# Group 1 of a graph attention layer by seven products instead of whole ones, with the sums of M on VectorE

## The reference

```python
h = jnp.maximum(_layernorm(x, axis=-1), 0.0)
output = jnp.einsum('bni,io->bno', h, weight)
q = jnp.einsum('bni,io->bno', h, wq)
k = jnp.einsum('bni,io->bno', h, wk)
alpha = jnp.einsum('bno,bmo->bnm', q, k)
alpha = jnp.maximum(alpha, 0.0) * (adj != 0)
alpha = jax.nn.softmax(alpha, axis=1)
x = x + jnp.einsum('bnm,bmo->bno', alpha, output)
```

## Time and profile before

| | |
|---|---|
| median of 3 runs | 415.41 us (415.18 to 416.22) |
| the profiled execution | 415.38 us, its span 413.5 us |
| granted TensorE clock, mean | 0.999 |
| busy: PE, DVE, ACT, POOL | 405.9, 297.0, 277.7, 264.7 us |
| start of scores(0), the first after group 0's products | 44.67 us |
| start of group 2's first product | 73.81 us |
| start of group 3's first product | 99.16 us |
| a later period | 23.6 us |

### The profile page before, as it was taken

One profiled execution on the slowest core, in us unless ns is written; L12 is line 12 of the kernel. 1 busy time (PEld: TensorE's weight loads), 2 busy tenths in 40 slices (PEclk: granted clock), 3 DMA queues, 4 the chain that ended last, 5 costly groups with the idle time before them and its releaser, 6 DMA issues.

```text
span 413.5 us, 9484 instructions
## 1 busy us (share of the span) xinstructions
PE 405.9 (98%) x3581; PEld 322.1 (78%) x3581; DVE 297.0 (72%) x569; ACT 277.7 (67%) x590; POOL 264.7 (64%) x284
## 2 busy tenths in 40 slices
PE   8999999999999999999999999999999999999995
PEld 5444545879798897979798797979889797979883
DVE  5799789596767777676767777676777667656465
ACT  4749877576767677776776776776867777643534
POOL 0749896969395875849486775939577584910003
PEclk9999999999999999999999999999999999999999
DMA  8973868978969797896979598796988699393022
GB/s 290 370 102 72 208 112 222 251 169 198 196 195 195 226 151 211 201 217 171 180 237 180 134 235 210 195 208 179 187 248 162 159 213 236 41 186 103 2 103 101
DMA packets 161641, 75.03 MB, mean 181 GB/s; under 512 B 135360, under 2 KB 143808, under 8 KB 161600
## 3 DMA queue, kind: packets, MB, share of 16 engines
q1 hardware_dynamic: 161312, 73.94, 77.9%
q10 hardware_dynamic: 288, 0.52, 0.3%
HBM read 24.12 MB, written 16.78 MB: 99 GB/s over the span
## 4 chain that ended last, share of the span: by engine, by line
PE 78%; DVE 7%; POOL 6%; ACT 6%; issue 2%; DVEq 0%; ACTq 0%
PE bank L1136 10%; PE bank L1139 10%; PE bank L1138 10%; PE bank L1153 9%; PE bank L1154 9%; PE bank L1151 9%; PE s_bank L1167 3%; PE s_bank L1166 3%; PE s_bank L1165 3%; PE bank L1172 2%; PE bank L1174 2%; PE bank L1173 2%; POOL hn_lo L423 2%; ACT h L543 2%; DVE raw_stats L828 1%
## 5 line engine op out<-in xcount | busy, mean ns | idle before, releaser
L423 POOL TENSOR_TENSOR hn_lo<-h,hn_hi 128x512 f16<-128x512 f32 x64 | 74.6, 1177 | 51.3 <-ACT hn_hi L553 51.2
L543 ACT ACTIVATE h<-x_sb,shift,rstd 128x512 f32<-128x512 f32 x64 | 49.9, 803 | 21.8 <-POOL shift L418 21.8
L449 POOL TENSOR_TENSOR hn_lo<-s,hn_hi 128x512 f16<-128x512 f32 x56 | 63.1, 1160 | 0.3 <-ACT hn_hi L558 0.3
L1138 PE MATMUL bank<-hT_lo,mt_hi 128*128 128x256 f16 x224 | 61.1, 273 | 0.0
L1136 PE MATMUL bank<-hT_hi,mt_hi 128*128 128x256 f16 x224 | 61.1, 273 | 0.0
L1139 PE MATMUL bank<-hT_hi,mt_lo 128*128 128x256 f16 x224 | 61.1, 273 | 0.0
L1153 PE MATMUL bank<-wt_lo,hT_hi 128*128 128x256 f16 x224 | 61.1, 273 | 0.0
L1151 PE MATMUL bank<-wt_hi,hT_hi 128*128 128x256 f16 x224 | 61.1, 273 | 0.0
L1154 PE MATMUL bank<-wt_hi,hT_lo 128*128 128x256 f16 x224 | 61.1, 273 | 0.0
L558 ACT ACTIVATE hn_hi<-s 128x512 f16<-128x512 f32 x56 | 33.7, 625 | 28.0 <-POOL s L438 23.1
L1136 PE MATMUL bank<-hT_hi,m_hi 128*128 128x256 f16 x168 | 45.8, 273 | 0.9 <-ACT bank L580 0.9
(11 more groups left out here) (166 smaller groups left out, 1104.7 us busy)
## 6 DMA issues: line engine op xcount, KB each, us to landing
out_h<-x_sb SPq DMA_DIRECT2D x63, 256.0 KB, 2.1
x_sb<-in_x SPq DMA_DIRECT2D x15, 1024.0 KB, 5.6
adj_sb<-in_adj SPq DMA_DIRECT2D x16, 256.0 KB, 5.4
hn_hi<-in_L_gnn_wq SPq DMA_DIRECT2D x4, 256.0 KB, 5.5
x_sb<-in_x SPq DMA_DIRECT2D x2, 512.0 KB, 7.1
w_sb<-in_L_gnn_weight SPq DMA_DIRECT2D x2, 512.0 KB, 8.7
hn_lo<-in_L_gnn_wk ACTq DMA_DIRECT2D x2, 256.0 KB, 4.0
hn_lo<-in_L_gnn_wk SPq DMA_DIRECT2D x2, 256.0 KB, 3.8
```

Of the source, the lines that this page charges most:

```text
L423: nc.gpsimd.tensor_tensor(hn_lo[:, s, b], h[:, b], hn_hi[:, s, b], ALU.subtract).then_inc(h_split, 1)
L449: nc.gpsimd.tensor_tensor(low, s32[:, f], high, ALU.subtract).then_inc(s_split, 1)
L543: nc.scalar.activation(h[:, b], x_sb[:, s, b], ACT.Relu, bias=shift[:, b:b + 1], scale=rstd[:, b:b + 1]).then_inc(h_made, 1)
L1138: nc.tensor.matmul(o, bh[:, k, cols], al[:, :, k], start=False, stop=False, skip_group_check=True)
```

## The change

Group 1 goes by seven products too (`FIRST = 1`). TensorE does those without sums first (P1 of t and v, then P2 of both), then P5 and P6 of t, P5 of v, P7 of t, P6 of v, the outs of group 0, P3 of t, P7 of v, P4 of t, P3 and P4 of v, and scores(1). GpSimd makes the sums of h of group 1 and its low parts as well, and all four sums of W ahead of the scales of group 1; VectorE makes the sums of M, in a buffer of their own. The buffers for P5 and c22 lie in w_sb, which is free by then. ScalarE and VectorE have a new order for group 1, and SP transposes group 1's sums. In group 2 the copy of P5 of v and two high parts of group 3's sums change places on ScalarE. Of the last five stores ScalarE's queue issues two. The core of the diff:

```diff
-    FIRST = 2
-    LOOPED = FIRST + 1
+    FIRST = 1
+    LOOPED = FIRST + 2
...
-        p5_t, p5_v, c22_t, c22_v = (spare[:, k].rearrange("p a b -> p (a b)") for k in range(4))
+        p5_t, p5_v, c22_t, c22_v = (w_sb[:, k] for k in range(4))
...
-        mt32 = spare
+        mt32 = sb("mt32", [N, 4, HK, HD], F32)
```

GpSimd's part, behind the first two sums of W:

```diff
-            layernorm_scales(1)
             pool.wait_ge(wt_summed, 1)
...
-            for b in range(GB):
-                lo_of_h(1, 1, b)
-
-            pool.wait_ge(m_copied, K)
...
+            layernorm_scales(1)
+            sums_of_h(1, 1)
             layernorm_scales(2)
...
+            lows_of_sums(1, 1)
+
+            pool.wait_ge(s_split, sums(2, 0))
+            sums_of_h(2, 0)
             lows_of_sums(2, 0)
```

ScalarE's part, the middle of group 1 and the last two stores:

```diff
+            hi_of_whole_v(3)
+            hi_of_mt(0)
+            hi_of_mt(1)
             normalise_h(2, 2, 0)
+            copy_p1_t(1)
             normalise_h(2, 2, 1)
+            copy_p1_v(1)
+            exponentials(0)
...
             hi_of_h(2, 0, 0)
+            hi_of_t11(1)
+            hi_of_p(0)
+            hi_of_mt(2)
...
             hi_of_h(2, 0, 1)
+            copy_p5_t(1)
...
+            act.wait_ge(last_added, 1)
+            act.dma_start(out_dram[:, GB * LAST:GB * LAST + 1, :],
+                          x_sb[:, LAST % UNROLL, 0:1]).then_inc(stored[LAST % UNROLL], 16)
+            act.wait_ge(out_read, B - 1)
+            act.dma_start(out_dram[:, B - 1, :HD], x_sb[:, LAST % UNROLL, GB - 1, :HD]).then_inc(stored[LAST % UNROLL], 16)
```

ScalarE's period of group 2:

```diff
                 copy_p1_v(g)
+                if isinstance(g, int) and g == FIRST + 1:
+
+                    hi_of_sum(3, 1, 2, S2)
                 copy_p5_v(g)
+                if isinstance(g, int) and g == FIRST + 1:
+                    hi_of_sum(3, 1, 3, S4)
                 hi_of_p(g - 1)
```

VectorE's part around the low parts that the products wait for (its first rows are in the first place below):

```diff
+            softmax_sum(0)
+            lo_of_t(1, 0, bank[TA][:], 0, 0)
+            lo_of_p(0, range(HG))
+            sum_x_t(1)
+            lo_of_p(0, range(HG, GB))
+            lo_of_wt(1)
+            lo_of_mt(2)
+            stats_all(3, 3, 0)
+            sum_x_v(1)
+            stats_all(3, 3, 1)
+            sum_c22_t(1)
+            residual(0, 0, 0)
+            lo_of_v(1, 0, bank[VA][:], 0, 0)
+            residual(0, 0, 1)
+            stats_all(3, 3, 2)
+            residual(0, 0, 2)
+            residual(0, 0, 3)
             lo_of_wt(2)
...
+            sum_c22_v(1)
+            lo_of_mt(3)
+            lo_of_t(1, 1, c22_t, 1, 1)
             stats_all(3, 3, 3)
```

TensorE's part, from P7 of t on:

```diff
+            pe.wait_ge(t_summed, done(1, 1))
+            pe.wait_ge(mt_split, T3 + 1)
+            product_t(1, N_P7, bank[TB][:], False)
+            pe.wait_ge(wt_split, T2 + 1)
+            product_v(1, N_P6, bank[VB][:], False)
+            outs(0)
+            product_t(1, N_P3, bank[TE][:], False)
+
+            pe.wait_ge(v_summed, done(1, 1))
+            pe.wait_ge(wt_split, T3 + 1)
+            product_v(1, N_P7, bank[VB][:], False)
+
+            pe.wait_ge(t_summed, done(1, 2))
+            pe.wait_ge(mt_split, T4 + 1)
+            product_t(1, N_P4, bank[TB][:], False)
```

## The result

The changed kernel takes 430.11 us in the median of 6 runs (428.91 to 432.5), the kernel before 415.63 on the same chip: a ratio of 1.0354 [1.0327, 1.0381]. The profiled execution took 428.91 us, its span is 427.1.

The account below looks back on a forecast made before the run. The prediction took TensorE, busy 98% of the span, as the bound, with no slack in steady periods. Group 1 +9.1, group 2 +3.2 and the end −0.4 gave +11.9 on 415.38: 427.3 us, range 423.0 to 430.5.

Parts of the forecast that it names:

- rival (c): TensorE's clock falls after the idle 3.6 us, costing 1.5 to 3 us more: 429.5 us; chance 0.10.
- scores(0): Start of group 1's stretch: the last tT_lo ends at 45.9 us, so scores start 1.3 us late.
- P5 of t: Group 1: waits for the transposed sums, landing at 55.7 us; loss 3.1 us, bounds 1.9 to 3.7.
- P7 of t: Group 1: waits for the third mt_lo on VectorE; loss 2.5 us, bounds 1.4 to 2.5.
- out of graph 3: Outs of group 0, within group 1: waits for residual(0), ready at 67.7 us; loss 1.1 us.
- P7 of v: Group 1: waits for the third wt_lo behind four residuals, until 73.3 us; loss 3.6 us, interference up to 1.2 more.
- P4 of t: Group 1: waits for the fourth mt_lo, ready at 76.2 us against 74.7; loss 1.6 us.
- Group 2's start: End of group 1: group 2 starts at 82.9 us against 73.81, +9.1 us.
- Group 2's waits: Group 2: copy of P1 waited for 1.4 us, p_lo 3.3; +3.2 us taken, bounds 0.4 and 4.
- The end: Last stores: one issued on ScalarE's queue, so the last goes sooner; −0.4 us, bounds 0 and −0.6.
- rival (b): No interference between VectorE and GpSimd, so waits in groups 1 and 2 shrink: about 423.5 us; chance 0.14.
- rival (a): Everything is covered: VectorE's list fits under TensorE's outs and P3, so the kernel gains, 412.3 us; chance 0.04.

Follow-up runs that it names:

- m_gpsimd: The changed kernel with the four sums of M made by GpSimd instead of VectorE; 440.77 us, ratio 1.0627.
- fill: The changed kernel with 15 unread matmuls of 512 columns on TensorE between P3 of t and P7 of v of group 1; 431.57 us.
- wt_early: The changed kernel with only the third wt_lo moved ahead of group 3's statistics on VectorE; 427.65 us, ratio 1.0306.
- stats_early: The changed kernel with group 3's x loaded before group 1's transposition and its statistics and first two h made earlier; median of four runs 434.06 us.
- lows_wait: The changed kernel with GpSimd's low parts of group 3's sums waiting until VectorE has made all p_lo of group 1; 432.17 us.
- copies_first: The changed kernel with the last two high parts of group 3's sums back ahead of group 2's copies on ScalarE; 432.18 us.
- w_sums_back: The changed kernel with W's last two sums back behind the scales of group 1 on GpSimd; 430.23 us.
- lows_early: The changed kernel with three low parts (third mt_lo, third wt_lo, fourth mt_lo) moved ahead on VectorE; 425.64 us, ratio 1.0239.
- lows_fill: The lows_early kernel with 13 unread matmuls of 512 columns in TensorE's wait for p_lo in group 2; 425.12 us by 425.64.
- stores_only: The kernel before with only the last stores changed, two of five issued by ScalarE's queue; 415.49 us against 415.5, ratio 1.000.

## Why the prediction was right, and where its numbers were off

The forecast was 427.3 us (423.0 to 430.5), measured 430.11. The loss lies where it was forecast, in TensorE's waits for low parts in groups 1 and 2. But the median is above the 425 to 429 us that had most of the chance, and inside the range by 0.4 us only, through the case of rival (c), whose figure was 429.5. In the order of the steps:

- *scores(0)*: 1.3 us late by forecast, 1.29 in the trace.
- *P5 of t*: forecast at 55.7, in the trace at 55.68. In m_gpsimd, where the transposition is later, it starts 5.1 us later, and the whole takes 10.7 us more: it is on the path.
- *P7 of t*: forecast 2.5, bounds 1.4 to 2.5; 1.35 in the profiled execution, 2.42 in fill, wt_early, stats_early, lows_wait, copies_first and w_sums_back. In all of them GpSimd's first sum of group 2 starts 0.3 or 0.4 us ahead of this mt_lo; here the sum is held (2.11 us, mt_lo 0.69), there mt_lo is (1.76). What decides which, the traces don't show. So the upper bound was the usual case, and the profiled execution the lucky one.
- *out of graph 3*: 1.1, and 0.90.
- *P7 of v*: 3.6, and with interference "up to 1.2 more"; 4.41 here, 3.62 in copies_first, lows_wait, m_gpsimd and w_sums_back. wt_early shows the place of wt_lo as its cause. That it starts at 73.29 here by a forecast of 73.3 is luck: the v_lo ahead of it came 1.0 us sooner than forecast (68.24 against 69.2), since mt_lo had been early, and the wt_lo took 0.84 us longer.
- *P4 of t*: 1.6, and 1.47.
- *Group 2's start*: forecast 82.9, and 85.38; 83.56 where the clock stayed up (copies_first). The term that the sum had at nothing is TensorE's clock: rival (c), which had a chance of 0.10, holds in this profile, at 2.5 us in group 1, and in the fill, lows_early, wt_early, stats_early and m_gpsimd profiles behind the wait for p_lo too. All six runs of the changed kernel have a mean clock of 0.98 to 0.99, and the slowest (432.5) the lowest; the kernel before has 0.999.
- *Group 2's waits*: p_lo 3.3, and 3.04, as forecast; the wait for the copy of P1 (1.4) did not come, since TensorE came 2.5 us later while ScalarE's chain did not. It came (1.1 us) in lows_early and lows_fill, where TensorE was 5.6 and 6.1 us sooner, and in fill, where the chain was 1.4 us later. Group 2 lost 27.33 − 25.35 = 2.0 us instead of 3.2. So two misses offset each other in part: 2.5 us too little in group 1, 1.2 too much in group 2.
- *The end*: −0.4 was wrong, 0 is measured (stores_only).
- *Small slips*: rival (b)'s sum is 427.3 − 1.1 − 1 − 2 = 423.2, not 423.5; group 2's own sum gives 3.6, and 3.2 was taken. Of VectorE's operations ahead of scores(0), tT_lo reads a bank and only one operand in SBUF, so not all have two SBUF inputs.

Group 3's first product comes out at 82.9 + 25.35 + 3.2 = 111.45 by the forecast and at 112.71 in the trace, 1.3 more; with the 0.4 of the end that is the 1.6 us between 427.3 and the profiled 428.91. The other 1.2 to the median are executions with a lower clock and, as far as the profiles of other kernels tell, the later mt_lo.

Rival (b), no interference, is refuted by the rows of 1.3 to 1.8 us in nearly every trace (and the four p_lo of group 2 took 3.5 us in the changed kernel, 1.11 before), and rival (a) by the result. Where the gain went: TensorE does less work here, since from scores(0) to group 2 the 39.40 us less 9.7 of waits and 2.5 of the clock leave 27.2, by 28.85 busy before. Of the 2.4 us forecast, 1.7 are seen so; TensorE's results come out 0.16 us late at each of the five waits, which comes to about the rest. But each product with a sum must have a low part first, and VectorE has these in a list with statistics, residuals and low parts of v. Moving three of them gives back 4.5 us, a new order of all lists 9.4, and neither makes the change pay. Whether an order exists that beats the kernel before stays open. The split of the loss between TensorE's own waits and the chain from group 3's statistics (theories A and B) is decided for A in group 2, by copies_first, lows_wait and lows_early; for group 1 it stays open how much of the lost clock reaches the end.

## What to carry to other kernels

A cheaper way to multiply is paid with operands that other engines must make. Before it is moved into the start of a program, write down for each product which low part it needs and what stands ahead of that part in its engine's list: the lists alone gave the six waits of group 1 to within 1.2 us. Removing one wait of 4.4 us gave some 2, since the next operand in the same queue was late as well; sum the chain, not the wait. And where the new waits are as long as the ones here, put a price on TensorE's clock behind them.

## What the runs showed of the hardware

- TensorE ran at half rate (0.43 us a matmul of 512 columns instead of 0.22) behind the wait for p_lo in fill (3.11 us), lows_early (3.11), wt_early (3.06), m_gpsimd (3.04) and stats_early (2.60), and at full rate behind 3.04 us in the changed kernel and 3.05 in w_sums_back. Behind the 3.62 us for wt_lo it ran at half rate in lows_wait and at full rate in copies_first; behind 2.11 us for the residual the next matmul ran at half rate in lows_fill and at full rate in lows_early, where the clock fell 1 us later. So the fall is no fixed price of a wait. Matmuls whose results nobody reads, put into the wait, went with a clock that stayed up in both kernels that had them (fill, and lows_fill with 0.22); since the clock can stay up without them, two profiles are a sign and no proof. The Trainium skill (TensorE: Matmul & The Clock Gate, Part 1) says that an idle engine drops to the lower clock; the trace agrees in kind.
- Behind a load of 1 MB on the same queue the issue of a transposition took 6.24 us (stats_early) instead of 3.40 (changed kernel).
- VectorE and GpSimd hold each other up, by up to 1.1 us an operation: in six kernels the third mt_lo took 1.76 us and GpSimd's sum beside it 1.5 or 1.65; in the changed kernel the mt_lo took 0.69 and the sum 2.11, where the next such sum took 1.26.
- With two of the last five stores on ScalarE's queue the median from issue to landing rose from 2.1 to 2.7 us, and the end stayed where it was (stores_only).
